# A cross-interaction recommender on one core: the order of transposes, top network and weight preparation rewritten

## What is computed

```python
def _L0_rec_ref(inputs, W0, W1):          # inputs: [1024, 32, 32]
    x, res = inputs, []
    for W in (W0, W1):
        prev = x.shape[1]
        z = einsum('bhd,bmd->bhmd', inputs, x).reshape(b, n * prev, k)
        x = einsum('bpd,pj->bjd', z, W)   # 128 outputs
        res.append(x)
    return sum(concatenate(res, axis=1), axis=-1)      # [1024, 256]

e = stack([tbl_f[ids[:, f]] for f in range(32)], axis=1)
z = _L0_rec_ref(e, W0, W1)
h = maximum(concatenate([z, dense_ctx], axis=1) @ W_top1 + b_top1, 0)   # 272 -> 512
h = maximum(h @ W_top2 + b_top2, 0)                                     # 512 -> 256
y = h @ W_top3                                                          # 256 -> 1
```

## Time and profile before

| | us |
|---|---|
| median of the runs (375.65 to 377.16) | 377.16 |
| the profiled execution | 377.52 |
| its span, first to last instruction | 375.7 |
| TensorE matmuls busy | 323.7 |
| VectorE busy | 203.2 |
| ScalarE busy | 233.9 |
| GpSimd busy | 252.3 |
| last gather starts | 332.5 |
| mean granted clock of TensorE | 0.982 |

### The profile page before, as it was taken

How to read it: one execution, slowest core, us unless ns; L and a number is a source line. 1 busy time by engine, 2 the same in 40 slices (tenths; PEclk the granted TensorE clock), 3 DMA queues, 4 the chain that set the end, 5 groups by cost and what they waited for, 6 DMA issues and landing times.

```text
span 375.7 us, 11560 instructions
## 1 busy us (share of the span) xinstructions
PE 323.7 (86%) x4680; PEld 298.8 (80%) x4680; DVE 203.2 (54%) x834; ACT 233.9 (62%) x774; POOL 252.3 (67%) x262
## 2 busy tenths in 40 slices
PE   1899936249998999899989998998699879989897
PEld 1677735248998999899989988988698878889797
DVE  4336999933665565555646663655455544554201
ACT  1578566187667766776686667666676557556601
POOL 5777887877777777777777777777777777740000
PEclk9999996699999999999999999999999999999999
DMA  7801001010100010000101000100010001100000
GB/s 220 312 14 16 11 9 16 9 16 14 16 16 16 14 16 16 16 16 15 16 13 17 15 17 15 15 15 15 15 16 14 16 15 17 15 10 2 3 2 0
DMA packets 10773, 9.79 MB, mean 26 GB/s; under 512 B 4664, under 2 KB 8896, under 8 KB 10720
## 3 DMA queue, kind: packets, MB, share of 16 engines
q0 software_dynamic: 8192, 4.21, 7.5%
q1 hardware_dynamic: 2528, 4.84, 3.8%
HBM read 9.03 MB, written 0.00 MB: 24 GB/s over the span
## 4 chain that ended last, share of the span: by engine, by line
POOL 66%; issue 21%; PE 10%; DMA 1%; ACT 1%; POOLq 0%; DVE 0%; SPq 0%
POOL emb L278 66%; PE WA L726 4%; PE M L739 1%; PE PA L687 1%; DMA emb<-in_table,rows 1%; PE QB L698 1%; DMA base<-in_bases 1%; PE M L758 1%; PE M L749 0%; POOLq L81 0%; ACT h L358 0%; PE T L711 0%; PE T L787 0%; PE M L750 0%; PE ET L787 0%
## 5 line engine op out<-in xcount | busy, mean ns | idle before, releaser
L278 POOL DMA_INDIRECT emb<-in_table,rows x256 | 251.6, 983 | 80.4 <-issue 77.8
L726 PE MATMUL WA<-TS,RX 128*128 128x128 f32 x896 | 111.0, 277 | 1.0 <-ACT TS L285 1.0
L726 PEld LDWEIGHTS WA<-TS,RX 128*128 128x128 f32 x896 | 104.6, 192 | 4.1 <-issue 4.0
L584 DVE COPY TS<-T 32x64 f32<-32x64 f32 x256 | 55.5, 217 | 76.7 <-PE T L711 69.7
L285 ACT ACTIVATE eblk<-ET 32x256 f32<-32x256 f32 x128 | 48.7, 380 | 55.3 <-PE ET L674 53.0
L687 PE MATMUL PA<-eblk,zP 128*128 128x132 f32 x512 | 75.0, 282 | 1.9 <-ACT TS L285 1.1
L552 DVE TENSOR_TENSOR zQ<-ET,eT 128x1024 f32<-128x1024 f32 x32 | 39.2, 1225 | 65.2 <-ACT eT L285 65.1
L285 ACT ACTIVATE TS<-T 32x64 f32<-32x64 f32 (+1 forms) x320 | 66.5, 208 | 7.7
L687 PEld LDWEIGHTS PA<-eblk,zP 128*128 128x128 f32 x512 | 66.7, 195 | 2.7 <-ACT TS L285 1.3
L546 DVE TENSOR_TENSOR zP<-ET,eT 128x224 f32<-128x224 f32 (+6 forms) x224 | 47.7, 289 | 0.0
L285 ACT ACTIVATE TS<-PA 128x396 f32<-128x396 f32 (+1 forms) x96 | 44.5, 463 | 2.7 <-PE PA L687 1.6
(11 more groups left out here) (87 smaller groups left out, 290.5 us busy)
## 6 DMA issues: line engine op xcount, KB each, us to landing
emb<-in_table,rows POOLq DMA_INDIRECT x256, 2.4
TS<-in_W SPq DMA_DIRECT2D x8, 256.0 KB, 5.6
wt<-in_W_top SPq DMA_DIRECT2D x2, 512.0 KB, 8.3
y1w<-in_W_rows SPq DMA_DIRECT2D x1, 448.0 KB, 6.7
TS<-in_W_rows SPq DMA_DIRECT2D x1, 448.0 KB, 7.3
sym<-in_W_cols SPq DMA_DIRECT2D x1, 264.0 KB, 3.0
TS<-in_W_cols SPq DMA_DIRECT2D x1, 264.0 KB, 3.3
idc<-in_ids SPq DMA_DIRECT2D x1, 128.0 KB, 2.1
```

Source lines behind the costliest of these rows:

```text
L278: eng.indirect_dma_start(emb[par][:, g, :], None, table, bass.IndirectOffsetOnAxis(rows[:, k, g:g + 1], 0))\
L584: eng.tensor_copy(view(ts[32 * q:32 * q + 32, :, :], P * REST + b0, [[4 * P, 2], [P, 4], [1, 8]]), view(src, q, [[C17, 2], [4, 4], [C33, 8 ...
L726: m = eng.matmul(WA[:, 0:P], C[:, kt, :], TS[k % 2][:, slot_of(kt), :], start=(kt == 0), stop=(kt == KT - 1))
```

## The change

It does five things.

- **Transposes.** `emb_transposes(u + 1)` moves from the head of unit u to its end, behind `other_triples(u)` (`ahead`). Units 0 to 2 are transposed during the weight steps (`EARLY_AT`). A unit's order becomes: `fill(u)`, across, the three trios, others.
- **Top network.** `fill(u)` puts pieces of `second(k - 1)` in front of unit u's triples: 9, 13, 19 and 15 in the four units; 16, 12, 16, 12 for tile 0; 18, 20, 18 and 0 for tile 6. `first` stands behind the last piece, `hidden1` at the end of unit 3, `hidden2` and `result` in units 0 and 1 of the tile after. For tile 6, `hidden1` stands in unit 31, `hidden2` behind it, `result` inside the last tile's `second`.
- **Weights.** The 56 pieces are transposed in place (RT, QC, TH), in another order of the pieces, in the units 4 to 7 between the pieces of `second(0)` that need them; the first four groups go through M and WA, the others through M alone. The sums are split by what they feed, with a semaphore each.
- **Pairs.** The 28 pairs of a part of eight fields lie in blocks of 4 x 4, twice 2 x 2 and 4 pairs, and no longer by distance: four instructions for zP and not seven, and for the sums too.
- **Copies.** ET is copied to eT first; eblk is then copied from eT (SBUF), and the products wait for eT alone. The rest copies are shared 1 : 3 between VectorE and ScalarE in tile 0 (units 0 to 3), 2 : 2 later.

```diff
+        BLOCKS = ((0, 0, 4), (HALF, 0, 2), (HALF + 4, 4, 2), (HALF + SUB, 0, 1))
-        C = RX[:, :, :].rearrange("p h (x l) -> p (h x) l", l=L)
+        KT_ORDER = [*range(HALF, F), *range(HALF), *range(F, KT)]
+        W_ORDER = (4, 5, 6, 7, 0, 1, 2, 3, 8, 9, 10, 11, 12, 13)
+        FIRST_UNIT = ((), (), (), (), (0, 1, 2, 3), (4, 5, 6, 7), (8, 9, 10, 11, 12), (13,))
+        def pieces(k):
+            if k == 0:
+                return (0, 16, 28, 44, KT)
+            if k == END - 1:
+                return (0, 18, 38, KT, KT)
+            return (0, 9, 22, 41, KT)
-        EARLY_AT = (8, 18)
+        EARLY_AT = (10, 20, F - 1)
+        def ahead(u):
+            if u == 1:
+                return 3
+            return u + 1 if 3 <= u < ALL - 1 else None
...
+            def e_copy(u):
+                eng.wait_ge(et_made, u + 1)
+                copy(eT[:, :], ET[:, 0:GROUPS * F]).then_inc(eT_made, 1)
-                    copy(dst, ET[r, 0:GROUPS * F].rearrange("p (g x h) -> p g x h", x=2, h=HALF)).then_inc(eblk_made, 1)
+                copy(dst, eT[r, :].rearrange("p (g x h) -> p g x h", x=2, h=HALF)).then_inc(eblk_made, 1)
...
-                for s in range(1, SUB) if second else range(0, SUB):
-                    n = SUB - s if s else 4
-                    dst = rt(HALF * (1 - X) + c0, 32 * (2 * X + e) + (off(s) if s else PAIRS), [[RTC, cn], [1, n]])
-                    h, other = (s, 0) if second else (0, s)
-                    add(dst, dst, rx(X, SUB * e + h, c0, SUB * e + other, cn, (1, n), (1,)), s_done)
+                for at, f, w in BLOCKS:
+                    dst = rt(row, col + at, [[RTC, cn]] + pairs_at(w))
+                    h, other = (f + w, f) if second else (f, f + w)
+                    by = (to_other, RAB) if second else (RAB, to_other)
+                    add(dst, dst, rx_at(X, SUB * e + h, c0, SUB * e + other, [[to_c, cn]] + steps(w, *by)), s_done)
...
             def across_triples(u):
+                eng.wait_ge(z_made, NZ * u + 1)
+                eng.wait_ge(eblk_made, NQ * (u + 1))
                 wait(eng, q_kept, 2 * u)
...
             def last_tile():
-                second(END, range(KT - 14))
+                second(END, 0, 24)
+                result(END - 1)
+                second(END, 24, F + HALF)
                 first(END)
-                second(END, range(KT - 14, KT))
+                second(END, F + HALF, KT)
...
+            for u in range(ALL):
+                fill(u)
+                across_triples(u)
+                for r in range(TRIOS):
+                    triples(TRIOS * u + r)
+                other_triples(u)
+                if UNITS < u < ALL - 1 and u % UNITS == UNITS - 1:
+                    hidden1(u // UNITS - 1)
+                if ahead(u) is not None:
+                    emb_transposes(ahead(u))
+            hidden2(END - 1)
             last_tile()
```

More of the change, by code:

```diff
@@ L24, with part_pairs @@
 Y1T = 7
-def off(s):
-    return sum(SUB - r for r in range(1, s))
+def part_pairs():
+    pairs = [(a, 4 + b) for a in range(4) for b in range(4)]
+    pairs += [(4 * n + a, 4 * n + 2 + b) for n in range(2) for a in range(2) for b in range(2)]
+    pairs += [(2 * j, 2 * j + 1) for j in range(4)]
+    return pairs
 def pair_columns():
@@ L408, in _ @@
+            hidden2(END - 1)
+            for j in range(by_vector(ALL - 1), NQ):
                 rest_copies(ALL - 1, j)
+            y_copy(END - 1)
             y1_copy(END)
@@ L446, in both_across, with steps @@
-            def both_across(X, c0, cn, second, s_done):
-                for s in range(1, SUB) if second else range(0, SUB):
-                    n = SUB - s if s else 4
-                    dst = rt(HALF * (1 - X) + c0, 64 * X + (off(s) if s else PAIRS), [[RTC, cn], [32, 2], [1, n]])
-                    h, other = (s, 0) if second else (0, s)
-                    add(dst, dst, rx(X, h, c0, other, cn, (SUB, 2, 1, n), (SUB, 1)), s_done)
+            def steps(w, by_first, by_second):
+                if w == 1:
+                    return [[2 * (by_first + by_second), 4]]
+                return [[by_first, w], [by_second, w]]
@@ L800, in _, with fill @@
                     emb_transposes(EARLY_AT.index(h))
-            for t in range(TOTAL):
-                u, r = divmod(t, TRIOS)
-                if r == 0 and len(EARLY_AT) <= u + 1 < ALL:
-                    emb_transposes(u + 1)
-                triples(t)
-                if r == TRIOS - 1:
-                    across_triples(u)
-                    other_triples(u)
-                if C_AT <= t < SLOTS_TILE:
-                    for q in range(C_TO[t - C_AT], C_TO[t - C_AT + 1]):
-                        weights(q)
-                if y2_range(t) is not None:
-                    second(*y2_range(t))
-                if tile_at(t, Y1_AT) is not None:
-                    first(tile_at(t, Y1_AT))
-                if tile_at(t, L1_AT) is not None:
-                    hidden1(tile_at(t, L1_AT))
-                if tile_at(t, L2_AT) is not None:
-                    hidden2(tile_at(t, L2_AT))
-                if tile_at(t, Y_AT) is not None:
-                    result(tile_at(t, Y_AT))
+            def fill(u):
+                k, i = divmod(u, UNITS)
+                if k >= 2 and i == 1:
+                    result(k - 2)
+                if u == ALL - 1:
+                    hidden1(END - 1)
+                if k == 0:
+                    return
+                n0, n1 = pieces(k - 1)[i:i + 2]
+                if k == 1:
+                    news = list(FIRST_UNIT[u])
+                    if i == 0:
+                        while news:
+                            weights(news.pop(0))
+                    while n0 < n1 or news:
+                        if news and (4 * W_ORDER.index(W_ORDER[news[0]]) <= n0 + 4 or n0 == n1):
+                            weights(news.pop(0))
+                        if n0 < n1:
+                            second(0, n0, n0 + 4)
+                            n0 += 4
+                else:
+                    second(k - 1, n0, n1)
+                if n1 == KT and n0 < KT or k == 1 and i == 3:
+                    first(k - 1)
+                if k >= 2 and i == 0:
+                    hidden2(k - 2)
```

400 lines of the change are left out of this document (231 added, 169 removed).

## The result

The changed kernel takes **378.8 us** in the median of nine runs (377.72 to 381.42); the kernel before, beside it, 377.01. Ratio 1.0065, 95% interval 1.0037 to 1.0093: slower by 0.65%, where 368.5 and a gain of 2.3% were predicted. The profiled execution (377.76 us, span 376.0, granted clock 0.968) is one of the shortest of the nine, where a span of 377.0 is commoner; and the ratio compares means, without one slow execution of the kernel before, 383.55 us.

The account below looks back on a forecast made before the run. GpSimd's gathers bound the kernel: span is the last gather's landing (334.9) plus TensorE's remaining work (40.8). The tail's gain of 8.6 us, all else zero, took the span from 375.7 to 367.1, so 368.5 us; range 365.0 to 371.8.

Parts of the forecast that it names:

- Item 4: Pairs by halves: fewer zP products and sums with RX, taken as zero, with 2 us each way for the range.
- rival C: Larger sums in tiles 0 and 1 shut GpSimd out longer; break-even at 8.6 us more stretch; chance 0.03.
- Item 1: Transposes at a unit's end: TensorE's work behind the last gather 10.1 us, before 19.1; gain 8.6 us.
- Item 2: TensorE through with unit 30 when the last gather lands: nothing counted, 0 to 1.5 us late in the range.
- rival A: TensorE late at unit 31, or handovers add up: 2 to 5 us, giving 370.5 to 373.5; chance 0.13.
- Item 3: Weights turned in place in tile 1: even 20 us more there is covered by 31 us; cost nothing.
- Item 5: ScalarE copies eblk from eT (SBUF), not ET (PSUM): left at 0; the skill's rule gave 0.04 us more a copy.
- The last gather starts more than 2 us away (B or C): Sign that the forecast is wrong: last gather off 332.5 by over 2 us, pointing to gathers beside the sums.
- B: Rival: fewer sums free the gathers, 3 to 5 us of stretch goes, giving 363.5 to 365.5; chance 0.11.
- the last transposes wait for nothing: Sign that the forecast is wrong: TensorE's last transposes no longer wait for gathers, pointing to a late TensorE or unshortened tail.

Follow-up runs that it names:

- e2_before_halves: The kernel before with only the pairs laid out by halves; 382.99 us, ratio 1.0152 to the kernel before.
- e8_gaps_between: Changed kernel with 28 VectorE waits, second-layer pieces between trios and one more VectorE rest copy in unit 30; 368.69 us, ratio 0.9786.
- e10_gap_per_12: Changed kernel with VectorE waiting for its own addition behind every twelfth one, 7 waits; 368.24 us in one execution.
- e3_wait_gaps: Changed kernel with VectorE waiting for its own addition behind every third one, 28 waits; 370.22 us, ratio 0.9802 to the kernel before.
- e11_gaps12_between: Changed kernel with 7 VectorE waits, second-layer pieces between trios and one more VectorE rest copy in unit 30; 368.92 us, ratio 0.9746.

## Why the prediction was wrong, by its steps

- *Item 4, the step that failed.* "I take zero", with 2 us each way, for the sums; they cost 7.5 us of gathers (259.1 against 251.6), and 7.4 us at the last gather. The mechanism is that of rival C, which had 0.03, and its break-even was well placed: the stretch was to grow by 8.6 us, and it grew by 7.5, from 9.2 to 16.7 above 242.4 (the prediction's 8.5 leaves out the first two gathers); TensorE's lateness did the rest. Two arguments were wrong. "The row nearest is that of the old sums" took the stretch as 0.3 us for each us of sums, 8.5 of 26.2, when what set it was where the held gathers were let in: with the old layout mostly at the small addition that ends a series, which the new layout does not have. And one gather of 2.12 us beside additions of 0.3 us was held against C, since the length of one addition is not the price; the same row said that a gather already waits for several additions in a row, and no row bounded how many. The upper bound of item 4, GpSimd shut out during all sums, 17.7 us, was computed, and then cut to 2 for the range without a row.
- *The rule.* The Trainium skill ("SBUF — State Buffer", SBUF: two separate sides) says that whoever starts first holds the shared pair for the whole instruction. Here a gather took 12.55 us beside 43 additions, none longer than 1.22 us (`e2_before_halves`): the measurement goes further than the rule, and decides.
- *Item 1, right.* Predicted: 10.1 us from the transposes to the second layer, measured 10.3; predicted stall 1.6 us, measured 1.38.
- *Item 2, mis-sized.* Predicted 39.9 us for units 27 to 30, measured 41.3 (302.29 to 343.63), so that TensorE was 1.4 us late instead of on time; and a middle tile took 36.7 us (126.31 to 163.04), not 34.9. The term is 16 x 0.1145 us for a unit's trios (rows of the trace, two to a matmul of the program): that was the price of `second`'s matmuls, and in the old order, with pieces between the trios, it was theirs too. The change itself puts the trios back to back, and there 16 take 2.18 us, 0.136 each in the mean; across takes 1.1 and not 0.99. The kernel before has a row with that price, in tile 0, where nothing stands between its trios. Timeline of TensorE in the kernel before, then in the changed kernel, unit 27:

```profile
42.69 2.22 PE L687 MATMUL PA<-eblk,zP 128*128 128x132 f32 x16 [0.78 <-ACT RX L285]
44.84 1.17 PE L698 MATMUL QB<-eblk,zQ 128*32 128x68 f32 x64
...
98.97 0.84 PE L687 MATMUL PA<-eblk,zP 128*128 128x132 f32 x6
99.65 1.72 PE L726 MATMUL WA<-TS,RX 128*128 128x128 f32 x14
```

```profile
308.67 2.25 PE L786 MATMUL PA<-eblk,zP 128*128 128x132 f32 x16
310.85 0.66 PE L815 MATMUL T<-eblk,z 128*32 128x132 f32 x16
```

  42.69 to 44.84 is 2.15 us for 16, 98.97 to 99.65 is 0.68 for 6, 308.67 to 310.85 is 2.18 for 16. In the last, 12 of the 15 steps from one to the next are 0.112 or 0.113 us; the excess sits behind the first matmul (0.217) and at the start of the third trio, which writes PA[0] again (0.191 and 0.216). These are handovers, as in rival A; that ScalarE's emptying of PA[0] causes the later one is argued, and fits with `e8_gaps_between`, where it is gone. With across it comes to 0.45 us a unit and 1.8 a tile, which is the whole difference for a middle tile. The range did allow 0 to 1.5 us late.
- *Item 3, right while the gathers bound.* TensorE is at unit 8 at 126.31 in place of 115.91, and still waits for gathers at units 23, 26 and 27: nothing was paid. The cover was smaller than computed, (40 - 36.7) x 6 = 20 us and not 31. With the gathers freed it is gone: `e10_gap_per_12`, 2.8 us earlier than `e3_wait_gaps` at unit 8 (120.64 for 123.42), is still 2.4 us earlier at unit 31 (334.12 for 336.56).
- *Item 5, where the rule was nearer than my row.* I left the cost of reading eT at 0, and the Trainium skill ("VectorE: DVE Perf Modes", The TRN2 errata) gave an estimated 0.04 us a copy, from its fixed 224 and 172 cycles. The group of eblk copies has a mean of 419 ns in the changed kernel and had 380 before: 0.04 us, so the trace agrees. Against 7.4 us it decides nothing.
- *What was to show it.* "The last gather starts more than 2 us away (B or C)" and "the last transposes wait for nothing" both came true. The first pointed to the gathers beside the sums, the second to item 2 (rival A), which had 1.4 us of the loss.

## What to carry to other kernels

When one engine's instructions are stretched beside another's, don't multiply a mean: list the stretched ones and see at which ends of the other engine they finish, and ask what the change does to the gaps between these. A run of VectorE additions with both inputs in SBUF, in which VectorE never stops, can hold a gather of GpSimd to its end, however short each addition is (7.37 us beside additions of at most 1.22). Seven waits that made VectorE stop lengthened 22 additions by 0.3 us and took 9.6 us off the span of the profiled execution (376.0 to 366.4). And when an edit frees the bound, recompute the engine behind it with its own durations: here TensorE stood 1 to 2 us behind, and took over.

## What the runs showed of the hardware

- A gather held to the end of a run is through 0.8 to 0.9 us after its last addition (41.48 after 40.64, 83.61 after 82.78, 77.48 after 76.64), close to the 0.94 it takes alone.
- What lets a gather into a run in which VectorE does not stop stays open: the number of additions, their size (16 or 32 elements), the layout and the operands don't settle it (beside additions inside RT a gather took 0.94 us at 34.85 in `e2_before_halves`, and one was held from 68.00 in the changed kernel), and `e10_gap_per_12` and `e11_gaps12_between`, with the same waits, differ by 2.5 us of gathers. That the additions' small shift against the gathers is the reason was not tried by itself.
- The cost of the waits was seen on VectorE: 22 additions in 5.84 us with none between them, 6.15 with a wait behind every twelfth and 6.74 behind every third.
